# State 4's first decay factor ahead of the silu stretch, the x and dt projections later on TensorE, B rows ahead of C rows, and DRAM pieces of 4 KB

## The chip, the cores and the metric

One NeuronCore of one Trainium2 chip. The metric is the device time of the whole program in microseconds (us), the median of the runs shown.

## The reference, cut to what matters

Four layers over 4096 tokens of 256 channels, each followed by a layer norm. The third is a selective state-space layer of 16 states, and the fourth a feed-forward net; the change is in these two and in the way their input passes through DRAM.

```python
# third layer: x of (tokens, 256)
x_ssm, z = split(x @ w_in.T + b_in)
z = silu(z);  dt = softplus(x_ssm @ w_dt.T + b_dt)
Bm = x_ssm @ w_B.T + b_B;  Cm = x_ssm @ w_C.T + b_C;  A = -exp(A_log)
for t:                                   # for each channel and each of the 16 states
    h = exp(A * dt[t]) * h + dt[t] * Bm[t] * x_ssm[t]
    y[t] = sum(h * Cm[t], axis=states)
x = layernorm(((y + D * x_ssm) * z) @ w_out.T + b_out + x) * gamma + beta, then a plain layernorm
# fourth layer
h = layernorm(x) * ln_gamma + ln_beta
x = layernorm(x + 0.5 * (silu(h @ w1 + b1) @ w2 + b2))
```

## The kernel before, in words

The program runs two layers in stages of their own (functions `first_layer` and `coupling`), and then the third and the fourth together, from about 520 us of the span on. This last stage works in 8 blocks (NB) of 512 tokens (TB). Each engine has its own program, written out by hand as a loop over `it` (L1649 for SP, L1887 for TensorE, L2151 for ScalarE, L2459 for VectorE, L2676 for GpSimd), with `cur = it` the block whose states are scanned now, `post` the one before, `last` and `old` those before that; `nxt` is the one whose projections are prepared. An engine takes its instructions strictly in the order written, and waits at each for the semaphore counts that it names. So the order of these calls is the schedule.

For each of the 16 states n of a block, and each half k of the channels (128 partitions):
- SP loads row n of B and row n of C from the DRAM array `CB_rows`, broadcast to all partitions (`load_B` L1620, `load_C` L1626), into 4 buffers each.
- GpSimd multiplies dt*x with the B row (`into`, L2560, 128x1024).
- ScalarE makes the decay factor exp(A*dt) into a PSUM bank `bank_a0` or `bank_a1` (`decay(b, n, k)`, L2021), copies the C row to a bank (`spread_C`, L2027) and saves the state's last column (`carry`, L2032).
- VectorE runs the recurrence (`scan(b, n, k)`, L2343, 128x512), and multiplies with C (`product(b, n)`, L2350, 128x1024); for n = 0, 12, 14 GpSimd makes that product.
- TensorE adds the products up over the states by transposes into `bank_y` (`add_up(b, n)`, L1762, 8 matmuls).

Besides, for each block, all in one PSUM bank, `single` (named bank_m1), in turn: `x_proj(b, m)` (L1710), evacuated by ScalarE's `evac_x(b, m)` (L2036), for m = 0, 1; `d_proj(b, m)` (L1720) with `evac_d(b, m)` (L2043), twice; `bc_proj` and `evac_bc`; then `z_proj` and `evac_z`, twice. Each projection waits until the one before it is evacuated. TensorE issues x_proj and d_proj of block cur between the add_ups of block post: x_proj(0) after add_up 0, x_proj(1) after 1, d_proj(0) after 2, d_proj(1) after 4. ScalarE has evac_x(0) after decay(4,0), evac_x(1) after decay(5,0), evac_d(0) after decay(6,1), and evac_d(1) at the head of the next turn of its loop (L2154), ahead of decay(8,0). On VectorE product(6) stands after scan(7,0), then come scan(7,1), scan(8,0), two `stats4` of the block before, product(7) and scan(8,1).

The silu stretch of ScalarE (L2263 to L2270) is two silus of the hidden layer `f_h` (128x2048 each), with spread_C(2) between them, and the silu of z; a table load stands ahead of it and one behind. `down_proj` (L1821) on TensorE takes `f_h` in eight parts, between the same add_ups. `stats4` (L2374) on VectorE needs GpSimd's `summed` (L2637), which adds `x2`, the block's input in token order, to the normed output. Into that same `x2` GpSimd's queue has added beta beforehand by a DMA with accumulation (`shifted`, L2577). The input itself goes to DRAM in the stage before, once in token order (`x2_tokens`, L1094) and once by channels (`x2_rows`, L1103), and comes back by `load_x2` (L1607) and `load_xT` (L1602).

## Time and profile before

| what | value |
| --- | --- |
| median of 3 runs | 1088.25 us (1087.13 to 1093.55) |
| profiled execution, its own time | 1091.2 us |
| its span, first to last instruction | 1089.2 us |
| mean granted TensorE clock | 0.966 of full speed |
| instructions | 17899 |

The busy time of an engine is a share of the span; the engines run side by side, so only a wait on the engine that ends a stage last makes the time longer. The numbers of a timeline are: start, duration, engine, line of the kernel, operation, output and input, and in brackets the idle time of the engine just before and what ended it. Durations of neighbours overlap by about 0.1 us, because an engine starts the next instruction while the last one drains. A row with "x2" holds two instructions of one kind, one after the other. The releaser in brackets is inferred.

### The profile page before, as it was taken

The numbers are of one execution on the slowest core, as the hardware profiler recorded it, in microseconds if no ns is written. First come the engines' busy times: TensorE is split into PE (matmuls) and PEld (weight loads), VectorE is DVE, ScalarE is ACT, GpSimd is POOL, SyncE is SP. The second block draws the span as 40 slices with busy tenths as digits, with TensorE's granted clock in tenths as the row PEclk, the third lists the DMA queues.
The fourth block names the chain that finished last, engine by engine and source line by source line (L and its number), as shares of the span: only waits on it lengthen the run. The fifth ranks groups of instructions, "written<-read, shape, count | busy, mean of one in ns | idle before, by whom it ended". The sixth has DMA issues, their size and how long they took to land. (4 is left out here: it accounts for less than half of the span.)

```text
span 1089.2 us, 17899 instructions
## 1 busy us (share of the span) xinstructions
PE 980.9 (90%) x5612; PEld 743.0 (68%) x5612; DVE 929.0 (85%) x1234; ACT 839.4 (77%) x1633; POOL 709.3 (65%) x603
## 2 busy tenths in 40 slices
PE   6999999999978999998668499999999989997987
PEld 4777777777754555555446387777778777886776
DVE  7999999999963797865799898999999899999751
ACT  7778878878746668767877789898998988987733
POOL 2556566766761111223789899999999899999530
PEclk9999999999998999999877799999999999999999
DMA  6543435433415002112998968588786978678301
GB/s 178 145 134 116 135 110 141 122 99 111 126 46 195 0 1 75 43 39 85 244 163 185 141 152 183 129 199 158 162 169 162 168 133 192 171 146 170 86 1 39
DMA packets 97617, 137.53 MB, mean 126 GB/s; under 512 B 8818, under 2 KB 52338, under 8 KB 97524
## 3 DMA queue, kind: packets, MB, share of 16 engines
q1 hardware_dynamic: 93828, 132.73, 50.2%
q0 software_dynamic: 3696, 3.67, 2.8%
q8 instruction: 45, 0.74, 0.3%
q14 instruction: 48, 0.39, 0.2%
HBM read 120.12 MB, written 14.16 MB: 123 GB/s over the span
## 5 line engine op out<-in xcount | busy, mean ns | idle before, releaser
L2348 DVE TENSOR_TENSOR_SCAN oa<-bank_a,h,oa 128x512 f32<-128x512 f32 x128 | 159.8, 1269 | 13.6 <-ACT h L2034 9.7
L2348 DVE TENSOR_TENSOR_SCAN ob<-bank_a,h,ob 128x512 f32<-128x512 f32 x128 | 160.0, 1268 | 8.0 <-ACT bank_a L2025 4.5
L1830 PE MATMUL bank_m<-w,f_h 128*128 128x256 f32 x448 | 104.4, 383 | 0.0
L1491 POOL TENSOR_TENSOR oa<-ob,x1T 128x1024 f32<-128x1024 f32 x8 | 18.8, 2355 | 130.5 <-DVE ob L1391 130.5
L2025 ACT ACTIVATE bank_a<-s,A 128x512 f32<-128x512 f32 x128 | 86.7, 683 | 21.2 <-DVE oa L2348 15.1
L2025 ACT ACTIVATE bank_a<-dtc,A 128x512 f32<-128x512 f32 x128 | 87.0, 684 | 13.7 <-DVE oa L2348 8.1
L1830 PEld LDWEIGHTS bank_m<-w,f_h 128*128 128x128 f32 x448 | 84.4, 192 | 14.1 <-issue 3.6
L1770 PE MATMUL bank_y<-ident,ob 128*128 128x128 f32 x512 | 71.7, 286 | 23.2 <-DVE ob L2354 11.8
L1770 PE MATMUL bank_y<-ident,oa 128*128 128x128 f32 x512 | 72.3, 288 | 17.7 <-DVE oa L2354 17.6
L1770 PEld LDWEIGHTS bank_y<-ident,ob 128*128 128x128 f32 x512 | 62.7, 148 | 34.5 <-DVE ob L2354 14.5
L2568 POOL TENSOR_TENSOR ob<-s,Bb 128x1024 f32<-128x1024 f32 x32 | 76.1, 2378 | 15.0 <-DMA Bb<-CB_rows 10.9
L1770 PEld LDWEIGHTS bank_y<-ident,oa 128*128 128x128 f32 x512 | 63.0, 149 | 29.1 <-DVE oa L2354 21.2
L2568 POOL TENSOR_TENSOR ob<-uc,Bb 128x1024 f32<-128x1024 f32 x32 | 76.1, 2377 | 10.2 <-DMA Bb<-CB_rows 6.5
L673 DVE TENSOR_TENSOR_SCAN L<-abc,zeros,b_id 128x512 f32<-128x512 f32 x64 | 78.3, 1265 | 4.6 <-POOL xd L883 3.6
L2568 POOL TENSOR_TENSOR oa<-uc,Bb 128x1024 f32<-128x1024 f32 x32 | 76.1, 2378 | 9.0 <-DMA Bb<-CB_rows 4.4
L883 POOL TENSOR_TENSOR xd<-xs,L 128x512 f32<-128x512 f32 x32 | 34.0, 1062 | 72.4 <-DVE xs L662 71.9
L2568 POOL TENSOR_TENSOR oa<-s,Bb 128x1024 f32<-128x1024 f32 x32 | 76.1, 2377 | 3.3 <-POOL ob L2575 2.1
L2354 DVE TENSOR_TENSOR oa<-ob,bank_c 128x1024 f32<-128x1024 f32 x64 | 77.3, 1207 | 0.9
L2030 ACT ACTIVATE bank_c<-Cb 128x512 f32<-128x512 f32 x104 | 61.6, 592 | 13.2 <-DVE ob L2354 8.2
L334 PE MATMUL b_op<-W_out,zs 128*128 128x256 f32 x256 | 63.1, 389 | 0.0
L2575 POOL TENSOR_TENSOR ob<-oa,Cb 128x1024 f32<-128x1024 f32 x24 | 57.2, 2383 | 2.7 <-PE bank_y L1770 2.7
L640 DVE SCALAR_TENSOR_TENSOR b_p<-raw,columns,b_p 128x512 f32<-128x512 f32 x72 | 54.2, 753 | 3.3 <-ACT b_p L465 1.7
(405 smaller groups left out, 2912.7 us busy)
## 6 DMA issues: line engine op xcount, KB each, us to landing
Bb<-CB_rows SPq DMA_DIRECT2D x128, 256.0 KB, 6.6
Cb<-CB_rows SPq DMA_DIRECT2D x128, 256.0 KB, 6.4
abc<-decays SPq DMA_DIRECT2D x32, 512.0 KB, 4.5
Ebc<-ramps SPq DMA_DIRECT2D x64, 128.0 KB, 3.1
uT<-in_uT SPq DMA_DIRECT2D x8, 512.0 KB, 4.2
u<-in_u SPq DMA_DIRECT2D x8, 512.0 KB, 3.9
x_tokens<-x2s SPq DMA_DIRECT2D x8, 512.0 KB, 3.2
x_rows<-x1T SPq DMA_DIRECT2D x8, 512.0 KB, 3.0
```

Source lines behind the costliest of these rows:

```text
L334: i = e.matmul(b_op[:, 0:DM], zs[b % 2][:, m, ts], W_out[:, m, :], start=(m == 0), stop=(m == MD - 1))
L640: e.scalar_tensor_tensor(to, raw[:, m, t:t + TB], cw[:, m, t:t + 1], acc[:, :], ALU.mult, ALU.add).then_inc(v_conv, 1)
L673: e.tensor_tensor_scan(L[:, hs, :].rearrange("p h t -> p (h t)"), abc[g % 2][:, hs, :].rearrange("p h t -> p (h t)"), b_id[:, :], zeros[:, ...
L883: e.tensor_tensor(heads(xd[:, :]), heads(xs[g % 2][:, :]), L[:, :, CH - 1:CH].to_broadcast([P, NH, HD]), ALU.mult).then_inc(p_xd, 1)
L1770: i = e.matmul(p_y[c // 2][:, at:at + P], prod[n % 2][:, k, c * CH:(c + 1) * CH], ident[:, :], start=False, stop=(n == NS - 1), is_transpo ...
L1830: i = e.matmul(to, f_h[:, k, c * CH:(c + 1) * CH], w2[:, k, :], start=False, stop=(c % 2 == 1 and k == KF - 1))
L2025: e.activation(p_a[k][:, :], dtc[b % 2][:, k, :], ACT.Exp, scale=A[:, k, n:n + 1]).then_inc(a_a, 1)
L2030: e.activation(p_c[:, :], Cb[n % 4][:, :], ACT.Copy).then_inc(a_c, 1)
L2348: e.tensor_tensor_scan(s[:, k, :], p_a[k][:, :], s[:, k, :], h0[:, n, k:k + 1], ALU.mult, ALU.add).then_inc(v_s, 1)
L2354: e.tensor_tensor(prod[n % 2][:, :, :], state[(NS * b + n) % 4][:, :, :], both(p_c[:, :]), ALU.mult).then_inc(v_g, 1)
L2568: e.tensor_tensor(state[at % 4][:, :, :], uc[b % 2][:, :, :], both(Bb[n % 4][:, :]), ALU.mult).then_inc(p_b, 1)
L2575: e.tensor_tensor(prod[n % 2][:, :, :], state[(NS * b + n) % 4][:, :, :], both(Cb[n % 4][:, :]), ALU.mult).then_inc(p_g, 1)
```

## The change

- **Decay factor.** In blocks 1 to 7 `decay(b, 4, 0)` is written to the bank `single` and issued before the silu stretch (`aside`, `factor`); `scan(b, 4, 0)` reads it there. It waits for the block's last evac_z. `decay(b, 5, 0)`, whose bank that leaves free, waits for scan(3,0) only. `x_proj(b, 0)` waits for that scan of the block before (b > 1).
- **Projections.** On TensorE x_proj(0) comes after add_up(2), x_proj(1) after add_up(3), d_proj(0) after add_up(4), d_proj(1) after add_up(6); the parts of `down_proj` stay where they are between the add_ups. On ScalarE evac_x(0) comes after decay(5,0), and evac_x(1) after decay(5,1); evac_d(0) and evac_d(1) stay.
- **DMAs.** `x2_tokens` and `x2_rows` in DRAM are laid out by partition, so that each partition's share of a block is one piece of 4 KB (before: 1 KB for tokens, 2 KB for rows); beta comes from an array in which it stands 4 times, again 4 KB. On SP load_x2 is issued before store_CB, and load_B(8), (9), (10) each one place earlier, ahead of load_C(6), (7), (8).
- The first fold_beta waits for c_xT, which x_proj did before.

```diff
@@ sync
                         load_C(post, 13)
+                        load_x2(post)
                     if 0 < cur < NB:
                         store_CB(cur)
...
-                    if live(post):
-                        load_x2(post)
...
                         load_B(cur, 7)
+                        load_B(cur, 8)
                         load_C(cur, 6)
-                        load_B(cur, 8)
+                        load_B(cur, 9)
                         load_C(cur, 7)
-                        load_B(cur, 9)
+                        load_B(cur, 10)
                         load_C(cur, 8)
-                        load_B(cur, 10)
                         load_B(cur, 11)
@@ sync, layouts
-                    e.dma_start(xT[:, :, :], x2_rows[:, :, b * TB:(b + 1) * TB]).then_inc(ld_xT, DMAS)
+                    e.dma_start(flat(xT), x2_rows[:, b, :, :].rearrange("p k t -> p (k t)")).then_inc(ld_xT, DMAS)
...
-                    e.dma_start(x2, x2_tokens[:, b * NC:(b + 1) * NC, :]).then_inc(ld_x2, DMAS)
+                    e.dma_start(flat(x2), x2_tokens[:, b, :]).then_inc(ld_x2, DMAS)
@@ new helpers
+            def aside(b, n, k):
+                return b > 0 and (n, k) == (4, 0)
+
+            def factor(b, n, k):
+                return single if aside(b, n, k) else p_a[k]
@@ tensor, x_proj
                         e.wait_ge(a_z, 2 * b)
+                        if b > 1:
+                            e.wait_ge(v_s, 2 * (NS * (b - 1) + 4) + 1)
@@ tensor, order
                         add_up(post, 0)
-                    if 0 < cur < NB:
-                        x_proj(cur, 0)
...
                         add_up(post, 1)
-                    if 0 < cur < NB:
-                        x_proj(cur, 1)
...
                         add_up(post, 2)
                     if 0 < cur < NB:
-                        d_proj(cur, 0)
+                        x_proj(cur, 0)
...
+                    if 0 < cur < NB:
+                        x_proj(cur, 1)
                     if 0 <= old < NB - 2:
                         down_proj(old, 1, 0)
                     if live(post):
                         add_up(post, 4)
                     if 0 < cur < NB:
-                        d_proj(cur, 1)
+                        d_proj(cur, 0)
...
                         add_up(post, 6)
+                    if 0 < cur < NB:
+                        d_proj(cur, 1)
@@ scalar, decay
-                    after(e, v_s, 2 * (NS * b + n - 1) + k + 1)
-                    e.activation(p_a[k][:, :], dtc[b % 2][:, k, :], ACT.Exp, scale=A[:, k, n:n + 1]).then_inc(a_a, 1)
+                    if aside(b, n - 1, k):
+                        e.wait_ge(v_s, 2 * (NS * b + n - 2) + k + 1)
+                    elif aside(b, n, k):
+                        e.wait_ge(a_z, 2 * b + 2)
+                    else:
+                        after(e, v_s, 2 * (NS * b + n - 1) + k + 1)
+                    e.activation(factor(b, n, k)[:, :], dtc[b % 2][:, k, :], ACT.Exp, scale=A[:, k, n:n + 1]).then_inc(a_a, 1)
@@ scalar, order
                         decay(cur, 3, 1)
+                    if 0 < cur < NB:
+                        decay(cur, 4, 0)
                     if 0 <= last < NB - 2:
                         silu_up(last, 0)
...
                         silu_z(cur)
-                    if live(cur):
+                    if cur == 0:
                         decay(cur, 4, 0)
+                    if live(cur):
+                        decay(cur, 4, 1)
                         carry(cur, 2)
+                        spread_C(cur, 3)
+                        carry(cur, 3)
+                        decay(cur, 5, 0)
                     if live(nxt):
                         evac_x(nxt, 0)
-                    if live(cur):
-                        decay(cur, 4, 1)
-                        spread_C(cur, 3)
-                        carry(cur, 3)
-                    if live(cur):
-                        decay(cur, 5, 0)
-                    if live(nxt):
-                        evac_x(nxt, 1)
                     if live(cur):
                         carry(cur, 4)
                         spread_C(cur, 4)
                         decay(cur, 5, 1)
+                    if live(nxt):
+                        evac_x(nxt, 1)
```

## Rows read from the trace of the kernel before

**Rows 1.** The page, busy times: us, share of the span, instructions.
```profile
PE 980.9 (90%) x5612; PEld 743.0 (68%) x5612; DVE 929.0 (85%) x1234; ACT 839.4 (77%) x1633; POOL 709.3 (65%) x603
```

**Rows 2.** Table by stretches, two blocks: length, busy per engine, clock, DMA.
```profile
719.30:782.70 63.40, 59.90 (x347) 48.86 (x346) 60.74 (x61) 57.35 (x103) 59.88 (x38) 1.00 0.79 164
846.20:911.50 65.30, 60.06 (x346) 48.73 (x345) 60.69 (x60) 57.30 (x102) 59.50 (x38) 1.00 0.85 163
```

**Rows 3.** VectorE's waits in the blocks from 719.3 and from 846.2.
```profile
DVE oa L2348 <- ACT h L2034: 1.4, 1, 1.4
...
DVE st L2376 <- POOL xl L2641: 2.5, 1, 2.5
```

**Rows 4.** Timeline of VectorE: scan(4,·), product(3), scan(6,0), product(6), scan(7,1), scan(8,0).
```profile
726.64 2.56 DVE L2348 TENSOR_TENSOR_SCAN oa<-bank_a,h,oa 128x512 f32<-128x512 f32 x2 [1.41 <-ACT h L2034]
729.12 1.20 DVE L2354 TENSOR_TENSOR oa<-ob,bank_c 128x1024 f32<-128x1024 f32 x1
...
733.73 1.26 DVE L2348 TENSOR_TENSOR_SCAN oa<-bank_a,h,oa 128x512 f32<-128x512 f32 x1
...
738.39 1.20 DVE L2354 TENSOR_TENSOR ob<-oa,bank_c 128x1024 f32<-128x1024 f32 x1
739.94 1.28 DVE L2348 TENSOR_TENSOR_SCAN ob<-bank_a,h,ob 128x512 f32<-128x512 f32 x1 [0.35 <-POOL ob L2568]
741.14 1.27 DVE L2348 TENSOR_TENSOR_SCAN oa<-bank_a,h,oa 128x512 f32<-128x512 f32 x1
```

**Rows 5.** Timeline of ScalarE: decay(3,·), silu, decay(4,0), decay(5,1), norm3, decay(7,1), evac_d(1).
```profile
716.71 1.30 ACT L2025 ACTIVATE bank_a<-s,A 128x512 f32<-128x512 f32 x2
...
719.32 1.92 ACT L2103 ACTIVATE f_h<-f_h 128x2048 f32<-128x2048 f32 x1
...
725.82 0.69 ACT L2025 ACTIVATE bank_a<-s,A 128x512 f32<-128x512 f32 x1
...
730.95 0.67 ACT L2025 ACTIVATE bank_a<-s,A 128x512 f32<-128x512 f32 x1
731.56 1.08 ACT L2077 ACTIVATE xl<-xl,nb,rs 128x256 f32<-128x256 f32 x2
...
739.14 0.67 ACT L2025 ACTIVATE bank_a<-s,A 128x512 f32<-128x512 f32 x1
739.75 0.66 ACT L2049 ACTIVATE dtc<-bank_m,columns 128x512 f32<-128x512 f32 x1
```

**Rows 6.** Timeline of TensorE: x_proj(1), add_up(2), d_proj(1), add_up(6).
```profile
727.26 1.98 PE L40 MATMUL bank_m<-s,w_xz 128*128 128x512 f32 x4 [1.41 <-ACT xc L2041]
729.08 1.04 PE L1770 MATMUL bank_y<-ident,ob 128*128 128x128 f32 x8
...
737.04 1.88 PE L40 MATMUL bank_m<-xc,w_dt 128*128 128x512 f32 x4
...
741.37 1.04 PE L1770 MATMUL bank_y<-ident,ob 128*128 128x128 f32 x8
```

**Rows 7.** Stretch of TensorE alone: length, busy, granted clock, DMA share, GB/s.
```profile
605.40:608.60 3.20, 3.18 (x4) 0.56 0.69 127
```

**Rows 8.** Timeline of TensorE, d_proj(1) in the block from 592.
```profile
605.42 3.37 PE L40 MATMUL bank_m<-xc,w_dt 128*128 128x512 f32 x4 [2.32 <-ACT dtc L2049]
```

**Rows 9.** Timeline of VectorE, stats4 in the block from 592.
```profile
616.36 1.30 DVE L2376 BATCH_NORM_STATS2 st<-xl 128x6 f32<-128x512 f32 x2 [4.85 <-POOL xl L2641]
```

**Rows 10.** Timeline of GpSimd, into(9) in the block from 592.
```profile
611.68 2.34 POOL L2568 TENSOR_TENSOR ob<-s,Bb 128x1024 f32<-128x1024 f32 x1 [3.42 <-DMA Bb<-CB_rows]
```

**Rows 11.** Timeline of VectorE, product(6) and scan(8,0) in the block from 532.
```profile
549.41 1.20 DVE L2354 TENSOR_TENSOR ob<-oa,bank_c 128x1024 f32<-128x1024 f32 x1
...
551.78 1.27 DVE L2348 TENSOR_TENSOR_SCAN oa<-bank_a,h,oa 128x512 f32<-128x512 f32 x1
```

**Rows 12.** DMA issues of the page: engine, count, KB each, median us to landing.
```profile
x_tokens<-x2s SPq DMA_DIRECT2D x8, 512.0 KB, 3.2
x_rows<-x1T SPq DMA_DIRECT2D x8, 512.0 KB, 3.0
```

More of the change, by code:

```diff
@@ L1012, in build @@
         ld_B, ld_C = [d_sem(f"ld_B{i}") for i in range(4)], [d_sem(f"ld_C{i}") for i in range(4)]
-        x2_tokens, x2_rows = scratch["x2_tokens"].rearrange("(n p) f -> p n f", p=P), rows(scratch["x2_rows"])
+        x2_tokens, x2_rows = scratch["x2_tokens"], scratch["x2_rows"]
         c_row, c_tok = new_sem("c_row"), [new_sem("c_tok0"), new_sem("c_tok1")]
@@ L1093, in sync @@
                     e.wait_ge(c_n, 4 * b + 4)
-                    e.dma_start(x2_tokens[:, b * NC:(b + 1) * NC, :], x2s[b % 2][:, :, :]).then_inc(c_tok[b % 2], DMAS)
+                    e.dma_start(x2_tokens[:, b, :], x2s[b % 2][:, :, :].rearrange("p c f -> p (c f)")).then_inc(c_tok[b % 2], DMAS)
                     if b == NB - 3:
@@ L1102, in sync @@
                     e.wait_ge(c_xT, 2 * b + 2)
-                    e.dma_start(x2_rows[:, :, tokens(b)], x1T[:, :, tokens(b)]).then_inc(c_row, DMAS)
+                    e.dma_start(x2_rows[:, b, :, :], x1T[:, :, tokens(b)]).then_inc(c_row, DMAS)
                     if b == NB - 2:
@@ L1539, in both @@
                 return x.rearrange("p (o t) -> p o t", o=1).to_broadcast([P, KD, TB])
-            beta_row = d["everywhere"].rearrange("(a o n) -> a o n", a=1, o=1)[:, :, sum(n for _, n in EVERYWHERE) - DM:]
+            beta_row = d["beta_rows"].rearrange("(a n) -> a n", a=1)
             def rowwise(v):
@@ L1746, in fold_beta @@
                 def fold_beta(part):
+                    if part == 0:
+                        e.wait_ge(c_xT, 2 * NB)
                     for m in (2 * part, 2 * part + 1):
@@ L2270, in scalar @@
                         silu_z(cur)
+                    if cur == 0:
+                        decay(cur, 4, 0)
                     if live(cur):
-                        decay(cur, 4, 0)
+                        decay(cur, 4, 1)
                         carry(cur, 2)
+                        spread_C(cur, 3)
+                        carry(cur, 3)
+                        decay(cur, 5, 0)
                     if live(nxt):
                         evac_x(nxt, 0)
-                    if live(cur):
-                        decay(cur, 4, 1)
-                        spread_C(cur, 3)
-                        carry(cur, 3)
-                    if live(cur):
-                        decay(cur, 5, 0)
-                    if live(nxt):
-                        evac_x(nxt, 1)
                     if live(cur):
@@ L2347, in scan @@
                     s = state[(NS * b + n) % 4]
-                    e.tensor_tensor_scan(s[:, k, :], p_a[k][:, :], s[:, k, :], h0[:, n, k:k + 1], ALU.mult, ALU.add).then_inc(v_s, 1)
+                    e.tensor_tensor_scan(s[:, k, :], factor(b, n, k)[:, :], s[:, k, :], h0[:, n, k:k + 1], ALU.mult, ALU.add).then_inc(v_s, 1)
                 def product(b, n):
@@ L2578, in shifted @@
                     e.wait_ge(v_pre, 2 * b + 2)
-                    e.dma_start(x2, beta_row.to_broadcast([P, NC, DM]), accum_op=ALU.add).then_inc(ld_beta, DMAS)
+                    e.dma_start(flat(x2), beta_row.to_broadcast([P, NC * DM]), accum_op=ALU.add).then_inc(ld_beta, DMAS)
                 def scales(parts, done, base):
@@ L2778 @@
         "columns": np.concatenate([column(down[n]) for n, _ in COLUMNS], axis=1),
+        "beta_rows": np.tile(a[L1 + "beta"], NC),
         "everywhere": np.concatenate([every[n].reshape(-1) for n, _ in EVERYWHERE]),
@@ L2784 @@
     out = nc.dram_tensor("out", (T, DM), F32, kind="ExternalOutput").ap()
-    scratch = {n: nc.dram_tensor(n, shape, F32, kind="Internal").ap() for n, shape in (("x2_tokens", (T, DM)), ("x2_rows", (DM, T)), ("CB_rows", (2 * NS, T)), ("decays", (NB * NC, DT, CH)), ("ramps", (NB * NC, DT, CH)))}
+    scratch = {n: nc.dram_tensor(n, shape, F32, kind="Internal").ap() for n, shape in (("x2_tokens", (P, NB, NC * DM)), ("x2_rows", (P, NB, KD, TB)), ("CB_rows", (2 * NS, T)), ("decays", (NB * NC, DT, CH)), ("ramps", (NB * NC, DT, CH)))}
     build(nc, dram, out, scratch)
```

## The prediction

> **What bounds the kernel now.** The whole page comes first: VectorE is busy for 85% of the span [rows 1], but that is a mean over four layers, and all of the reordering lies in the last one, which starts at about 520 us. So the second view is the table by stretches. One block of that layer (512 tokens) takes 63.4 us, and in it TensorE works 59.9, VectorE 60.7, ScalarE 57.4 and GpSimd 59.9 us [rows 2]. Four engines are nearly full; the longest, VectorE, has only 2.7 us to spare. The block from 846 us is 1.9 us longer. The third view, VectorE's waits, says where: 1.4 us before `scan(4,0)` in every block, and 2.5 us before `stats4` in the long one [rows 3].
>
> Fourth, the timelines of one block, that of 719 us. VectorE is idle for 1.41 us before the two scans of state 4 at 726.64 [rows 4]. ScalarE's row explains it: from 718.0 it is in the silu stretch (a table load, two silus of `f_h`, the silu of z, a table load back) and only at 725.82 does it write state 4's first decay factor [rows 5]. It hardly rests afterwards. The second small wait of VectorE, 0.35 us before `scan(7,1)` at 739.94, is put down to GpSimd, but the scan starts 0.13 us after ScalarE ends `decay(7,1)` (739.14 + 0.67), so it is ScalarE's. Fifth, TensorE [rows 6]: `x_proj(1)` at 727.26, `d_proj(1)` at 737.04, `add_up(6)` at 741.37. The four projections share one bank with their evacuations: x_proj(0), evac_x(0), x_proj(1), evac_x(1), d_proj(0), evac_d(0), d_proj(1), evac_d(1), strictly in turn. Now `d_proj(1)` is complete at 738.9 and ScalarE takes it at 739.75: 0.8 us in hand. That chain is what the change moves later.
>
> **The decay factor.** `decay(4,0)` goes ahead of the silus. It needs a slot of 0.61 us on ScalarE, so all up to its old place is 0.61 us later, and `decay(4,1)` starts at 726.44 and ends at 727.13. `scan(4,0)` goes at 725.2 (726.64 - 1.41), ends 726.5; `scan(4,1)` waits until 727.26; `product(3)` starts at 728.45 instead of 729.12. This part alone gives 0.67 us, not 1.41. It can't give more by `scan(7,1)`: from 718 to 739.8 ScalarE has 0.62 us of idle time, and its work isn't less.
>
> **The x and d projections.** The sum, for the same block; a semaphore from VectorE to TensorE or ScalarE costs 0.03 to 0.09 us, ScalarE to VectorE 0.13, a projection delivers 2.0 us after its first matmul when it had to wait (1.98 in [rows 6]), an `add_up` takes 0.87 in a full stream, eight matmuls of `down_proj` 1.73.
> Step 1: `x_proj(0)` now waits for `scan(4,0)`: it starts at 726.5 and delivers at 728.5; `evac_x(0)` ends at 729.15. ScalarE had got there at 728.4: nothing lost yet.
> Step 2: TensorE does `down_proj(0,1)` to 730.0, `add_up(3)` to 730.9 (product(3) is there at 729.7), then `x_proj(1)`, delivered at 732.95.
> Step 3: ScalarE, in order, reaches `evac_x(1)` at 730.9 and stands for 2.05 us. Behind it stand norm3, decay(6,0), and all else: norm3 starts at 733.54 instead of 731.56 [rows 5]. `decay(6,0)` ends at 735.2, and `scan(6,0)` starts at 735.33 instead of 733.73: the gain is gone and 1.6 us are lost.
> Step 4: ScalarE has no slack to 739.8, so it stays 2.0 late: `product(6)` at 740.26 instead of 738.39, ending 741.47. `d_proj(0)`, after `add_up(4)`, delivers at 737.37, when ScalarE just gets there: no further loss.
> Step 5: `d_proj(1)` now stands behind `add_up(6)`, which needs product(6): 741.53, then 0.87, then 2.05 to deliver (744.45), `evac_d(1)` 0.57, `decay(8,0)` 0.68, 0.13. `scan(8,0)` starts at 745.84 instead of 741.14: 4.7 us per block. The reason is one of order: ScalarE has `evac_d(1)` ahead of `decay(8,0)`, and on VectorE only one scan lies between product(6) and scan(8,0). From the end of product(6) the round trip is 4.35 us, the scan covers 1.2.
>
> After scan(8,0) the order and the gaps are as before; the two waits left (0.5 us at the softplus, 0.2 at the gate) follow VectorE and stay.
>
> By blocks: the one of 532 us (no silu_up, no new wait): the x loop makes product(6) about 1.1 us late and the round trip adds 3.2 (scan(8,0) was 2.37 after product(6) [rows 11]), 4.3; less 0.3 for earlier B rows, 4.0. The one of 592: scan(8,0) would come at 615.3 and end at 616.5, but VectorE waited for stats4 until 616.36 anyway, 4.85 us [rows 9]: of the loss 0.7 is left (scan(9,1), which follows the softplus). Those of 656, 719, 782 and 911: 4.7 each, 18.8. The one of 846: its wait of 2.5 us for stats4 vanishes and the 0.5 at the softplus returns: 4.7 - 2.0 = 2.7. The last, 975, has no projections to come: it keeps the first part, -0.5. Sum: 4.0 + 0.7 + 18.8 + 2.7 - 0.5 = 25.7 us.
>
> **The DMAs.** Rows of B ahead of C: GpSimd stood 3.42 us for Bb before `into(9)` in the block of 592 [rows 10], which made most of the 4.85. Both this and the 2.5 us are covered by the new lateness, so I cost the order at nothing; without that cover it would give up to 4.85 + 2.5. `load_x2` moves ahead of `store_CB` and of the first B rows on SP; its semaphores are long up there, its issue takes some 0.4 us, and the first B rows of the next block then have half a megabyte less in front of them. Larger pieces: half a megabyte of 1 KB pieces lands in 3.2 us and one of 2 KB in 3.0 [rows 12]; doubling gave 0.2. One more doubling or two on x2, xT and beta, none of which ended a wait but beta's perhaps in `summed`: 0 taken, bounds -2 (the 532 block, where GpSimd waits for B behind these stores) and +0.5 (if longer pieces hold a ring against the B rows). The Trainium skill, page "DMA: Bandwidth & Descriptors", section Specifications, asks for pieces of at least 512 B for line rate; by that the change of pieces would be worth nothing at all, while the row gives the 0.2 us per doubling. The sum is the same with either.
>
> **Sum and its base.** The profiled execution took 1091.2 us (span 1089.2): 1091.2 + 25.7 = 1116.9. The median of the runs is 2.95 us lower, so the forecast is 1088.25 + 25.7 = 1114 us, up 2.4%.
>
> **The rivals.**
> First, the wait goes and the projections stay hidden. Per block 0.6 x 6, and the stats4 waits go too (4.85 + 1.9), and 1 us of DMA: -11.3, 1077 us. For it: 1.41 us of idle time is plain to see. Against it: `d_proj(1)` cannot start before product(6), and decay(8,0) stands behind it in ScalarE's program. It would need the round trip to be under 1.2 us, and the rows say 4.35.
> Second, only the last loop costs. If TensorE brings x_proj(1) in time (from about 731 on), step 3 falls away; product(6) would be up to 0.6 us early, scan(8,0) at 743.3: 2.1 per block, 0.1 in that of 846, 2.6 in the first: +10.6, 1099 us. For it: TensorE's ends are modelled. Against: add_up(3) can't start before product(3), 729.7, and the rest is 2.9 us of work.
> Third, TensorE's clock falls besides. After the new round trip TensorE has caught up and stands about 2.5 us before `add_up(8)`. In the block of 592 it stood for 2.32 us, and the four matmuls after took 3.37 us [rows 8] where 1.98 is usual, at a mean granted clock of 0.56 [rows 7], that is mostly at 1.2 GHz. That costs up to 1.4 us of TensorE's time per block, in a stretch where it also waits for others; if it all counts in 6 blocks, +8.4: 1122 us. Against: at 752 to 755 it also idles today and the clock stays. The Trainium skill, "TensorE: Matmul & The Clock Gate", section What's actually happening, says that the slow clock is the default and that activity lifts it; by it the same would happen after each new pause.
>
> **How the numbers follow.** Forecast 0.63; clock 0.17; last loop only 0.15; hidden 0.05. The range leaves out the last case and the edges: 1098 to 1124. About 1% (10.9 us) is what this kernel's measurement can tell from no change. Faster by over 1%: 0.04, from the hidden case. Within 1%: 0.06, from a third of "last loop only" and a little of hidden. Slower by over 1%: 0.90.
>
> **What would show it.** In the profile after: blocks of about 68 us from 656 on; no wait before scan(4,0); a new idle of ScalarE of about 2 us before xc (evac_x(1)) and of about 2.7 us before dtc (evac_d(1)), both released by TensorE; VectorE waiting about 2.3 us before scan(6,0) and 2.7 before scan(8,0); no wait for xl in stats4. Wrong, if ScalarE takes evac_d(1) without a wait, or if the blocks stay at 63 us.

## The result, and the profile after

The kernel after takes 1125.88 us (median of 4 runs, 1124.15 to 1126.19) against 1090.38 us of the kernel before (1087.13 to 1093.55): ratio 1.032, 95% interval [1.0296, 1.0344]. It is slower by 35.5 us. The forecast was 1114 us with a range of 1098 to 1124: the direction was right, but a rise of 25.7 us was forecast and 35.5 was measured. (The median lies 11.9 us above the forecast. 2.1 us of that come from its base, the median of three runs; a fourth run of the kernel before moved it from 1088.25 to 1090.38.)

The page of the kernel after: its span, and the busy times that answer to [rows 1].

```profile
span 1123.2 us, 17899 instructions
...
PE 999.5 (89%) x5612; PEld 751.9 (67%) x5612; DVE 930.8 (83%) x1234; ACT 838.2 (75%) x1633; POOL 705.4 (63%) x603
```

The work of VectorE and ScalarE is that of before to 2 us; they stand longer. TensorE is the one with more busy time (999.5 against 980.9 us) for the same 5612 instructions, so some of them ran slower. The table by stretches (length, busy time with count of TensorE, its weight loads, VectorE, ScalarE and GpSimd, granted clock, DMA share, GB/s) for the first three blocks and three later ones; the fourth and the sixth row answer to the two of [rows 2]:

```profile
532.50:599.90 67.40, 49.28 (x251) 39.35 (x250) 54.96 (x51) 42.63 (x78) 49.93 (x22) 0.75 0.74 164
599.90:671.90 72.00, 56.20 (x296) 42.48 (x295) 62.07 (x58) 55.32 (x99) 60.79 (x42) 0.86 0.67 148
671.90:741.00 69.10, 63.22 (x346) 50.77 (x345) 59.91 (x59) 55.27 (x99) 56.95 (x35) 0.95 0.58 146
...
741.00:808.90 67.90, 62.34 (x346) 49.83 (x345) 60.95 (x61) 57.42 (x103) 58.27 (x37) 0.97 0.67 157
808.90:876.80 67.90, 62.25 (x346) 49.52 (x345) 60.94 (x61) 57.41 (x103) 58.27 (x37) 0.97 0.66 155
876.80:946.20 69.40, 63.74 (x347) 50.98 (x346) 61.34 (x61) 57.41 (x104) 58.22 (x37) 0.95 0.65 152
```

A usual block (those from 741.00, 808.90 and 946.20 here) is 67.9 us instead of 63.4. VectorE's busy time in it is unchanged (60.95 against 60.74), so the 4.5 us are waiting. Where it waits, the view of its waits says (us in total, times, longest), block from 808.9; [rows 3] had 1.4 us before scan(4,0) here:

```profile
DVE oa L2363 <- ACT bank_a L2039: 4.6, 2, 2.5
DVE ob L2363 <- ACT bank_a L2039: 1.1, 2, 0.5
DVE oa L2363 <- ACT h L2048: 0.9, 1, 0.9
DVE zgs L2375 <- PE bank_y L1779: 0.2, 1, 0.2
```

The timelines give each its place. VectorE: scan(6,0), product(6), scan(7,1), scan(8,0), as in [rows 4].

```profile
820.08 1.28 DVE L2363 TENSOR_TENSOR_SCAN oa<-bank_a,h,oa 128x512 f32<-128x512 f32 x1 [2.08 <-ACT bank_a L2039]
...
824.94 1.22 DVE L2369 TENSOR_TENSOR ob<-oa,bank_c 128x1024 f32<-128x1024 f32 x1
826.67 1.28 DVE L2363 TENSOR_TENSOR_SCAN ob<-bank_a,h,ob 128x512 f32<-128x512 f32 x1 [0.51 <-ACT bank_a L2039]
830.47 1.28 DVE L2363 TENSOR_TENSOR_SCAN oa<-bank_a,h,oa 128x512 f32<-128x512 f32 x1 [2.51 <-ACT bank_a L2039]
```

ScalarE: evac_x(1), evac_d(0), evac_d(1), as in [rows 5].

```profile
817.71 0.69 ACT L2055 ACTIVATE xc<-bank_m,columns 128x512 f32<-128x512 f32 x1 [1.90 <-PE bank_m L40]
...
822.10 0.68 ACT L2063 ACTIVATE s<-bank_m,columns 128x512 f32<-128x512 f32 x1
...
829.07 0.69 ACT L2063 ACTIVATE s<-bank_m,columns 128x512 f32<-128x512 f32 x1 [2.53 <-PE bank_m L40]
```

TensorE: add_up(6), d_proj(1) and add_up(8), as in [rows 6].

```profile
826.21 1.09 PE L1779 MATMUL bank_y<-ident,ob 128*128 128x128 f32 x8 [0.86 <-DVE ob L2369]
827.14 1.88 PE L40 MATMUL bank_m<-xc,w_dt 128*128 128x512 f32 x4
...
839.43 1.57 PE L1779 MATMUL bank_y<-ident,ob 128*128 128x128 f32 x8 [2.39 <-DVE ob L2369]
```

Read from product(6): VectorE writes it from 824.94 to 826.16, TensorE adds it up at once, projects to 829.02, ScalarE evacuates at 829.07 and makes the decay factor at 829.65, and VectorE, which has only scan(7,1) to do meanwhile, has stood 2.51 us when it starts scan(8,0) at 830.47. Two round trips that were hidden before are now on the path: this one, and that through x_proj(1), for which ScalarE stands 1.90 us. scan(4,0) itself no longer waits; the 0.9 us in the view of the waits stand before scan(4,1).

Per block, measured from the start of one silu of z to the next (the last entry runs to the end of the span), the kernels compared below have these lengths. The labels are those of the experiments. The blocks have the names that they have in the prediction; from 656 on the silu of z starts some 4 us behind the name (at 660.5, 723.5 and so on in the kernel before). The columns 719, 782 and 846 are the blocks from 741.0, 808.9 and 876.8 of the kernel after. Each row is one profiled execution, so a difference that shows in one row alone may be one of executions.

```
kernel       532    592    656    719    782    846    911  975 to end   span
before      59.40  68.25  62.97  63.42  63.43  65.37  63.43  110.1     1089.2
after       67.37  71.98  69.14  67.89  67.90  69.33  67.92  109.1     1123.2
e1_order    69.79  71.33  67.96  68.18  68.15  68.17  68.17  110.1     1126.1
e2_dma      63.49  64.00  62.95  63.40  63.42  63.40  63.41  110.0     1088.4
e3_d1       65.33  67.64  64.18  65.30  65.28  65.29  65.30  109.0     1101.3
e4_fill     69.50  75.64  67.41  67.90  67.92  67.90  67.88  108.9     1125.5
e5_first    61.28  64.34  67.40  67.90  67.90  67.90  67.89  110.6     1108.5
e6_x1       63.83  65.40  63.55  65.30  65.30  65.31  65.29  109.0     1095.6
e7_pieces   63.42  63.95  62.96  63.42  63.40  63.42  63.40  110.3     1088.2
e8_sp       62.79  65.38  62.95  63.41  63.42  63.41  63.42  111.7     1089.1
e9_tight    59.66  65.24  62.63  63.43  63.44  63.44  63.44  109.1     1083.0
e10_fill    67.12  67.75  67.41  67.91  67.90  67.91  67.91  110.5     1116.9
```

### The profile page after: what moved, and what is told of

It reads as the page before. It is cut to its first block and busy times, and to the rows that moved or that the text cites. A ratio compares the mean times of both kernels' runs of the same rounds, so it can differ in the third digit from the quotient of the medians.

```text
span 1123.2 us, 17899 instructions
## 1 busy us (share of the span) xinstructions
PE 999.5 (89%) x5612; PEld 751.9 (67%) x5612; DVE 930.8 (83%) x1234; ACT 838.2 (75%) x1633; POOL 705.4 (63%) x603
## 2 busy tenths in 40 slices
DMA packets 87889, 137.53 MB, mean 122 GB/s; under 512 B 8818, under 2 KB 40562, under 8 KB 87796
## 5 line engine op out<-in xcount | busy, mean ns | idle before, releaser
L2363 DVE TENSOR_TENSOR_SCAN oa<-bank_a,h,oa 128x512 f32<-128x512 f32 x121 | 151.5, 1272 | 45.9 <-ACT bank_a L2039 34.2
L1779 PE MATMUL bank_y<-ident,ob 128*128 128x128 f32 x512 | 76.4, 298 | 44.6 <-DVE ob L2369 33.1
L1779 PEld LDWEIGHTS bank_y<-ident,ob 128*128 128x128 f32 x512 | 64.3, 153 | 57.6 <-DVE ob L2369 41.4
L2039 ACT ACTIVATE bank_a<-s,A 128x512 f32<-128x512 f32 x124 | 84.1, 685 | 14.4 <-DVE oa L2363 8.8
L1779 PE MATMUL bank_y<-ident,oa 128*128 128x128 f32 x512 | 75.5, 296 | 19.9 <-DVE oa L2369 19.5
L1779 PEld LDWEIGHTS bank_y<-ident,oa 128*128 128x128 f32 x512 | 64.3, 153 | 35.8 <-DVE oa L2369 32.8
```

The lines of the kernel that those rows point to most:

```text
L1779: i = e.matmul(p_y[c // 2][:, at:at + P], prod[n % 2][:, k, c * CH:(c + 1) * CH], ident[:, :], start=False, stop=(n == NS - 1), is_transpo ...
L2039: e.activation(factor(b, n, k)[:, :], dtc[b % 2][:, k, :], ACT.Exp, scale=A[:, k, n:n + 1]).then_inc(a_a, 1)
L2363: e.tensor_tensor_scan(s[:, k, :], factor(b, n, k)[:, :], s[:, k, :], h0[:, n, k:k + 1], ALU.mult, ALU.add).then_inc(v_s, 1)
```

## The experiments

They ran in three series (e1 to e4, e5 to e8, e9 and e10), each on another chip and each with runs of the kernel before among them. Every ratio is against the kernel before of its own series.

**The order of the projections alone (e1_order).** The kernel before with the projections later on TensorE and ScalarE; decay(4,0) stays behind the silus, no bank is borrowed, the DMAs are as before.

```diff
                         add_up(post, 0)
-                    if 0 < cur < NB:
-                        x_proj(cur, 0)
...
                         add_up(post, 2)
                     if 0 < cur < NB:
-                        d_proj(cur, 0)
+                        x_proj(cur, 0)
...
                         add_up(post, 6)
+                    if 0 < cur < NB:
+                        d_proj(cur, 1)
```

> The kernel before with the later x and dt projections alone (TensorE's and ScalarE's order of them; no decay factor in the shared bank, DMAs as before). Theory 1, the order of the projections makes the whole loss: about 5 us per full block (4.7, and 0.35 more because product(3) is later without the early factor), as much in the first block as after the change: 1127 us (1120 to 1132). Rival, the loss comes from the shared bank, x_proj(0) waiting for scan(4,0): under 1100 us.

Measured: 1126.27 us (before in these runs 1092.6), ratio 1.0312, interval [1.0279, 1.0345]. The order makes the whole loss; the shared bank and the DMAs are not needed for it. Its usual block is 68.17 us, 0.27 longer than that of the kernel after: that is all that the early factor is worth there (the DMA parts, the other difference, leave the usual block at 63.4, see e2_dma). As the expectation said, the first block loses at least as much as after the whole change, 10.4 us against 8.0.

**The DMA parts alone (e2_dma).** New layouts, beta array and SP's order, nothing else.

```diff
-                    e.dma_start(x2, x2_tokens[:, b * NC:(b + 1) * NC, :]).then_inc(ld_x2, DMAS)
+                    e.dma_start(flat(x2), x2_tokens[:, b, :]).then_inc(ld_x2, DMAS)
```

> The kernel before with the DMA parts alone (4 KB pieces, rows of B ahead of C, load_x2 earlier). Theory 1: nothing is lost, and without the cover of the late projections the waits of stats4 in the blocks of 592 and 846 us go, 4.8 and 1.9 us: 1083 us (1080 to 1090). Rival 2, that the excess of 3.4 us in the block of 532 us over the forecast is GpSimd waiting longer for B (3.69 us after, 2.93 before, ahead of into(4)): 1092 us or more, and that wait over 3.5 us.

Measured: 1088.42 us, ratio 0.9961, interval [0.9943, 0.998]. The waits for stats4 went in both places (68.25 to 64.00, 65.37 to 63.40), but the first block became 4.1 us longer (59.40 to 63.49). GpSimd waits longer there before into(4), for the first row of B that was not loaded in the stage before. This is its timeline in this kernel; the wait was 2.93 us in the kernel before:

```profile
537.44 2.35 POOL L2567 TENSOR_TENSOR oa<-uc,Bb 128x1024 f32<-128x1024 f32 x1 [4.24 <-DMA Bb<-CB_rows]
```

So of the rival the wait came true (over 3.5 us) and the time did not. Over the first two blocks the sum is that of before (127.5 against 127.7), and only the 2 us of the block from 846 are left; in this execution the first block also starts 1.4 us later.

**d_proj(1) ahead of the trip through product(6) (e3_d1).** The kernel after, with that one projection two places earlier.

```diff
                         add_up(post, 5)
+                    if 0 < cur < NB:
+                        d_proj(cur, 1)
...
                         add_up(post, 6)
-                    if 0 < cur < NB:
-                        d_proj(cur, 1)
```

> The kernel after, with d_proj(1) ahead of add_up(6) (behind add_up(5)). Theory 1, the round trip through product(6): ScalarE no longer stands before evac_d(1) (2.5 us now), the full blocks shrink from 67.9 to 65.2 us, the first two by about 3 as well: 1107 us (1103 to 1112). If the loss were in x_proj(1) alone: within 3 us of the kernel after.

Measured: 1103.09 us, ratio 1.0093, interval [1.0062, 1.0125]. The usual block falls from 67.9 to 65.3, as expected to 0.1. The span falls by 21.9 us, more than 2.6 per block, because the blocks from 592, 656 and 846 shrink by 4.3, 5.0 and 4.0 us; that from 532 shrinks by 2.0.

**x_proj(1) earlier besides (e6_x1).** As e3_d1, and

```diff
+                    if 0 < cur < NB:
+                        x_proj(cur, 1)
                     if live(post):
                         add_up(post, 3)
...
                     if 0 <= post < NB - 1:
                         norm3(post, 0)
+                    if live(nxt):
+                        evac_x(nxt, 1)
```

> The kernel after with d_proj(1) behind add_up(5) (as in the run e3_d1), and besides x_proj(1) ahead of add_up(3) on TensorE, with evac_x(1) behind the first norm3 on ScalarE. My theory: the loss of 4.5 us per full block has two terms, the trip through product(6), which the earlier run took away (67.9 to 65.3), and ScalarE's stand of 1.9 us before evac_x(1), which this one takes away: full blocks at 63.4 (63.0 to 63.8), 1103.1 - 5 x 1.9 = 1093.6 (1090 to 1098). Rival: the remaining 1.9 us is TensorE's lower clock and its dips, or ScalarE's stand moves on to evac_d(0); then the blocks stay at 65 or more and the time above 1100.

Measured: 1097.4 us, ratio 1.0032, interval [1.0017, 1.0046]. A miss: the usual block stays at 65.3. ScalarE's wait for x_proj(1) is gone, but ScalarE's timeline shows what took its place, the next link of the chain, evac_d(0):

```profile
803.87 0.69 ACT L2063 ACTIVATE s<-bank_m,columns 128x512 f32<-128x512 f32 x1 [1.78 <-PE bank_m L40]
```

1.90 us of waiting became 1.78, because d_proj(0) still stood behind a part of down_proj and add_up(4). It was the second half of the rival, though the time stayed under its 1100. Of the 5.7 us that were gained 4.4 are in the first three blocks; the rest is in front of them, where this execution starts its first block 1.4 us earlier.

**Each projection as early as the borrowed bank allows (e9_tight).** All parts of the change; order of before in the first two blocks; from the third on, against the kernel after,

```diff
                         down_proj(old, 0, 1)
+                    if 2 < cur < NB:
+                        x_proj(cur, 1)
                     if live(post):
                         add_up(post, 3)
...
-                    if 0 < cur < NB:
-                        x_proj(cur, 1)
+                    if 2 < cur < NB:
+                        d_proj(cur, 0)
...
                         add_up(post, 4)
                     if 0 < cur < NB:
-                        d_proj(cur, 0)
+                        d_proj(cur, 1)
```

> All parts of the change, but the projections brought only as late as the borrowed bank forces: the first two blocks in the order of before (factor of block 1 in its old place); from the third on x_proj(0) behind add_up(2), x_proj(1) behind the next part of down_proj and ahead of add_up(3), d_proj(0) behind add_up(3), d_proj(1) behind add_up(4); evac_x(1) on ScalarE behind the first norm3. The run with d_proj(1) and x_proj(1) moved had blocks of 65.3 us, with ScalarE standing 1.78 us for d_proj(0) and VectorE 1.67 us before scan(7,0). My theory: that stand is the last one of the chain; with d_proj(0) one add_up earlier ScalarE no longer waits and the early factor's gain of 0.6 us per block comes out: full blocks 62.8 (62.6 to 63.4), first two 61.3 and 64.3 as in the run e5_first; 1111.5 - 5 x 5.1 = 1086 us (1083 to 1090) against about 1092 of before, ratio 0.994. Rival: the early factor gives nothing, since ScalarE's work in the block is the same and VectorE's waits only move; then the blocks take 63.4 or more and the time is 1089 or more, no better than the DMA parts alone.

Measured: 1087.96 us (12 runs; before in these 1090.1), ratio 0.9977, interval [0.9961, 0.9993]. The loss is gone: in the usual block ScalarE waits for no x or dt projection by more than 0.2 us. But that block is 63.44, not 62.8. So the two waits for projections together carry the 4.5 us of the usual block, and the gain by the early factor, 0.6 us per block in my sum, does not exist: the rival was right, and the kernel is no better than the DMA parts alone (0.9961). VectorE's waits in the usual block, here from 786:

```profile
DVE ob L2378 <- ACT bank_a L2045: 1.1, 2, 0.5
DVE oa L2378 <- ACT h L2054: 0.9, 1, 0.9
DVE oa L2378 <- ACT bank_a L2045: 0.2, 1, 0.2
DVE zgs L2390 <- PE bank_y L1779: 0.2, 1, 0.2
```

They add up to 2.4 us; before, the same view of the block from 786.9 has 1.4, 0.5, 0.4 and 0.2, 2.5 in all. The 1.4 us before scan(4,0) are spread over scan(4,1) (0.86), scan(6,0) (0.23) and scan(7,1) (0.51 instead of 0.35).

**The old order in the first two blocks only (e5_first).** The kernel after, in which the projections of blocks 1 and 2 stand as before.

```diff
                         add_up(post, 0)
+                    if cur in (1, 2):
+                        x_proj(cur, 0)
...
-                    if 0 < cur < NB:
+                    if 2 < cur < NB:
                         x_proj(cur, 0)
```

> The kernel after, in which only the projections that run beside the first two blocks of the last stage (those of blocks 1 and 2) keep the order of before, on TensorE and ScalarE, and block 1's factor stays in its old place. The two blocks take 67.4 and 72.0 us in the kernel after; with the DMA parts alone they take 63.5 and 64.0. My theory: what my forecast missed lies in these two blocks, and it is the chain of the projections that starts later there, so they return to about 63.5 and 64.0 and all others stay as in the kernel after: 1125.9 - 3.9 - 8.0 = 1114 us (1110 to 1118). Rival: the excess of the two blocks is TensorE's cold start or the DMAs and not the order; then they stay at 66 to 72 and the time is above 1120.

Measured: 1111.46 us, ratio 1.0165, interval [1.0137, 1.0194]. Expected 1114. The two blocks return to 61.3 and 64.3, 13.7 us in all, so what they lost came with the order too. Besides, the block from 656 takes 67.40 instead of 69.14, at a granted clock of 1.00 instead of 0.95, and that from 846 67.90 instead of 69.33, at 0.97 instead of 0.95, though nothing was changed in them: those 1.4 to 1.7 us are not the order itself, and can be there in one execution and not in another.

**A filled TensorE, first try (e4_fill).** The kernel after with 8 dummy passes ahead of add_up(0) in the first block and 8 ahead of add_up(2) in the second.

```diff
+                    if cur == 2:
+                        e.wait_ge(v_pre, 2)
+                        fill(pair[1], 8)
                     if live(post):
                         add_up(post, 2)
```

> The kernel after with 8 matmuls of 128x512 added on TensorE ahead of add_up(0) of the first block and 8 more ahead of add_up(2) of the second, into banks not read before the next start; they only keep TensorE busy where it stood 5.85 and 1.94 us. Theory 3, the excess of the first two blocks over the forecast (3.4 and 3.0 us) is TensorE at 1.2 GHz in the projections: those blocks shrink by 3 to 6 us in all, x_proj(0) of the second block takes 1.9 instead of 3.4 us, 1121 us (1118 to 1123). Rival, the excess is the order itself at any clock: within 1 us of the kernel after.

Measured: 1130.49 us, ratio 1.0343, interval [1.0309, 1.0378]. A miss, and no answer: the dummies were far too long. TensorE's timeline of this kernel shows those of the second block; x_proj(0), which took 3.46 and 3.41 us in the two blocks of the kernel after, took 1.88 in the first here:

```profile
603.97 7.03 PE L1763 MATMUL bank_m<-w_xz 128*128 128x512 f32 x16
```

7 us of filler in a gap of 1.94 us cost more than the clock gave, and so did 9.4 us in the gap of the first block, where d_proj(1) then ran slowly instead (3.20 us). Behind the second block there are no dummies, and still the blocks from 656 and 846 take 67.4 and 67.9 us at a clock of 1.00, after the same pause of 2.39 us before add_up(8) as in the kernel after.

**The same with two dummies in each of the gaps (e10_fill).** Ahead of add_up(8) from the second block on, and in the second block ahead of add_up(2) and add_up(6).

```diff
+                    if 1 < cur < NB:
+                        e.wait_ge(a_d, 2 * cur + 2)
+                        fill(single, 2)
                     if live(post):
                         add_up(post, 8)
```

> The kernel after with two dummy passes (512 columns each, into a bank that is free then, results not used) ahead of add_up(8) in the blocks from the second on, where TensorE stands 2.4 us, and in the second block also ahead of add_up(2) (stood 1.9 us) and add_up(6) (stood 2.4 us). Theory: the 1.2 to 1.4 us by which the blocks of 672 and 877 exceed the usual 67.9 (69.1 and 69.3, granted clock 0.95 in both) and some 3 us of the second block (its d_proj(1) took 3.6 us instead of 1.9) are TensorE's lower clock after such idle stretches; filled, the clock stays, those blocks come to 67.9 and 69 to 70: 1125.9 - 5.5 = 1120 us (1118 to 1123). Rival: the clock falls off the path; the time stays within 1 us of 1125.9.

Measured: 1120.13 us (before in these runs 1090.1), ratio 1.0277, interval [1.0254, 1.03]. Work was added, and against the kernel before the ratio is 1.0277 where the kernel after had 1.032 (the intervals share 0.0004). The stretches of the blocks from 592, 656 and 846:

```profile
599.60:667.40 67.80, 57.39 (x309) 42.04 (x308) 62.12 (x58) 55.36 (x99) 60.83 (x42) 0.95 0.69 157
667.40:734.80 67.40, 62.33 (x351) 49.33 (x349) 59.61 (x59) 55.44 (x100) 56.94 (x35) 1.00 0.59 150
870.60:938.50 67.90, 62.58 (x351) 49.44 (x350) 60.95 (x60) 57.48 (x104) 58.25 (x37) 1.00 0.65 154
```

They are 4.2, 1.7 and 1.4 us shorter than in the kernel after, at clocks of 0.95, 1.00 and 1.00 instead of 0.86, 0.95 and 0.95. For the block from 592 the dummies are the likely cause: x_proj(0), d_proj(1) and the add_ups between them are all fast in it. For the other two it is not shown, because these blocks had the short length and the full clock in e4_fill too, without a dummy. What speaks for the dummies there is that in all four runs the mean clock of the whole span is 0.965 to 0.967, while it is 0.951 to 0.953 in the four of the kernel after.

**The pieces alone, and SP's order alone (e7_pieces, e8_sp).** The two halves of e2_dma, each on the kernel before.

```diff
-            beta_row = d["everywhere"].rearrange("(a o n) -> a o n", a=1, o=1)[:, :, sum(n for _, n in EVERYWHERE) - DM:]
+            beta_row = d["beta_rows"].rearrange("(a n) -> a n", a=1)
```

> The kernel before with the new DRAM layouts (4 KB pieces for x2, xT and beta) alone, without the new order of SP. The DMA parts together made the first block 4.1 us longer (GpSimd's wait for the first B rows went from 2.9 to 4.2 us) and took away the waits for stats4 in the blocks of 592 and 846. The changed order of SP cannot act before the first B rows, so my theory: the first block's 4 us come from the pieces, 63.5 us here, and the block of 592 stays within 1 us of 68; 1092 + 4 = 1094 us (1090 to 1098). Rival: the pieces also take the waits away, and this kernel is as fast as both together, 1088.

```diff
                         load_C(post, 13)
+                        load_x2(post)
...
+                        load_B(cur, 8)
                         load_C(cur, 6)
-                        load_B(cur, 8)
```

> The kernel before with SP's order alone (load_x2 ahead of store_CB and of the first B rows; B rows 8, 9 and 10 one place earlier), old DRAM layouts. My theory: the first block stays at 59.4 to 60 us, and the waits before stats4 in the blocks of 592 and 846 go: 68.3 to 64 and 65.4 to 63.4. 1090.4 - 6 = 1084 us (1081 to 1088), ratio 0.994. Rival: the first block loses its 4 us here too, so they belong to the queue's order or to chance, and the time is 1088.

Measured: pieces 1088.61 us, ratio 0.9947 [0.9929, 0.9965]; SP's order 1090.03 us, ratio 0.9966 [0.9948, 0.9983]; before in these runs 1094.56. Both expectations failed in part. The pieces alone take both waits for stats4 away, which I had put down to SP's order; against the kernel before of their series they give 5.9 us. SP's order alone takes away the wait of the block from 846 and about halves the other. What is left of its 4.8 us, in the view of VectorE's waits, with the pieces alone:

```profile
DVE st L2376 <- POOL xl L2641: 0.2, 1, 0.2
```

With SP's order alone:

```profile
DVE st L2375 <- POOL xl L2640: 2.7, 1, 2.7
```

And the first block is longer in both, 63.4 and 62.8, so it isn't the pieces as such. What makes it 59.4 in the kernel before, 59.7 in e9_tight (which has all the DMA parts) and about 63 in the three DMA kernels was not settled. The traces differ in one more thing there: in e2_dma and e7_pieces, but not in e8_sp, e9_tight or the kernel before, TensorE stood 1.5 us before the block's x_proj(0) for its load from `x2_rows`. In the three DMA kernels the second block is short where the first is long. The two gains do not add: both together gave 0.9961.

## Why the prediction was right in direction and wrong in size

The forecast's terms against what was measured, in us over the kernel before; the third column is e10_fill, in whose trace most of the drops of the clock are missing.

```
block          forecast   after   e10_fill
532                4.0      8.0       7.7
592                0.7      3.7      -0.5
656                4.7      6.2       4.4
719, 782, 911      4.7 each 4.5 each  4.5 each
846                2.7      4.0       2.5
975 to the end    -0.5     -1.0       0.4
start of the first  -      -0.3      -0.4
sum               25.7     34.0      27.7
```

The forecast failed in two terms. The x loop of the first block was put at 1.1 us and measured 4.5; and TensorE's clock, put at nothing in the sum, made most of what the blocks from 592, 656 and 846 are above it (3.0, 1.5 and 1.3 us). The rest of the sum was too high by 1.4 us.

- **The bound and the two round trips (steps 1 to 5): right.** 4.7 us were forecast, 4.5 measured. By single waits: 2.05 us before evac_x(1), measured 1.90; 2.7 before evac_d(1), 2.53; about 2.3 before scan(6,0), 2.08; 2.7 before scan(8,0), 2.51; about 2.5 of TensorE before add_up(8), 2.39. e3_d1 took the second trip away, for 2.6 of the 4.5 us; e9_tight took away the rest. (That scan(4,0) waits 1.4 us "in every block" is not so: the view of the waits has 2.6 us in the block from 656 and no such wait in the first two. The sum of 656 did not suffer by it.)
- **The term that failed most in size: the block from 532, "the x loop makes product(6) about 1.1 us late and the round trip adds 3.2", 4.0.** The block lost 8.0. VectorE's timeline in it, kernel after:

```profile
553.65 1.19 DVE L2369 TENSOR_TENSOR ob<-oa,bank_c 128x1024 f32<-128x1024 f32 x1
...
559.12 1.28 DVE L2363 TENSOR_TENSOR_SCAN oa<-bank_a,h,oa 128x512 f32<-128x512 f32 x1 [3.02 <-ACT bank_a L2039]
```

  The block starts at 532.55 here and started at 532.84 before, so product(6) comes 21.1 us behind the start instead of 16.6 [rows 11]: 4.5 us late, not 1.1. From it to scan(8,0) are 5.5 us instead of 2.4: the round trip adds 3.1, as forecast. So it is the x loop that was mis-sized; I took its slack from the usual block. ScalarE stood for x_proj(0), x_proj(1) and d_proj(1) in turn:

```profile
543.35 0.69 ACT L2055 ACTIVATE xc<-bank_m,columns 128x512 f32<-128x512 f32 x1 [3.92 <-PE bank_m L40]
...
547.60 0.69 ACT L2055 ACTIVATE xc<-bank_m,columns 128x512 f32<-128x512 f32 x1 [2.37 <-PE bank_m L40]
...
557.74 0.69 ACT L2063 ACTIVATE s<-bank_m,columns 128x512 f32<-128x512 f32 x1 [4.37 <-PE bank_m L40]
```

  That is 10.7 us of standing, where the kernel before had 3.2 for the projections in this block (2.1 before xc and 1.1 before s in the view of ScalarE's waits). The longest of the first two, 3.92 us, is for x_proj(0). TensorE had stood 5.85 us for GpSimd's product(0) and starts add_up(0) only at 531.39. In the new order two more add_ups and two parts of `fold_beta` (small matmuls that come in this block alone) stand ahead of x_proj(0), and TensorE does them all at the lower of its two levels. Its stretch from there to the end of x_proj(0), kernel after (granted clock 0.51):

```profile
531.40:543.10 11.70, 11.70 (x46) 9.75 (x46) 7.58 (x7) 6.21 (x9) 6.56 (x3) 0.51 0.98 217
```

  x_proj(0) starts at 539.76 instead of 533.78. The 0.3 us that I took off for earlier B rows did not come either: GpSimd waits 3.69 us before into(4) instead of 2.93. How much of this wait the clock makes and how much the order, no run separates: e4_fill had the fast clock there but delayed the add_ups by its own dummies. With the old order and the same DMA parts product(6) comes 16.8 us behind the start in e5_first, but 20.7 in e2_dma, where GpSimd waits longer for its row of B. So the order's share of the 8.0 is not known to better than the 4 us by which this block differs among kernels that have the old order in it (59.4 to 63.5 us).
- **The clock: "Third, TensorE's clock falls besides" was a rival at 0.17, and it came true in part, on top of the forecast.** It was priced at up to 1.4 us in each of 6 blocks. Between the traces of the kernel after and of e10_fill lie 4.2 us in the block from 592, 1.7 in that from 656, 1.4 in that from 846 and nothing in the other full blocks. (The first block, whose slow stretch is the one above, got no dummies in e10_fill.) So the forecast for the block from 592 (0.7) failed by the clock: in e10_fill that block is 0.5 us shorter than before. TensorE's timeline there, kernel after:

```profile
619.45 1.97 PE L1779 MATMUL bank_y<-ident,ob 128*128 128x128 f32 x8 [2.39 <-DVE ob L2369]
621.21 3.62 PE L40 MATMUL bank_m<-xc,w_dt 128*128 128x512 f32 x4
```

  add_up(6) and d_proj(1), both inside the new round trip, take 5.4 us instead of the 2.8 of the usual block (826.21 to 829.02), and ScalarE, VectorE and scan(8,0) wait for all of it. Elsewhere the drop comes after add_up(8), off the path, and costs only where it lasts. Stretches of the kernel after: behind add_up(8) in the block from 808.9 and in that from 876.8.

```profile
839.40:843.20 3.80, 3.66 (x28) 2.48 (x28) 3.80 (x7) 3.27 (x7) 3.04 (x2) 0.57 0.70 154
907.30:914.70 7.40, 6.84 (x43) 5.46 (x44) 7.40 (x10) 5.89 (x14) 6.41 (x4) 0.56 0.73 215
```

  Both are near the lower level of 1.2 GHz; 3.8 us of it cost nothing (block 67.9), 7.4 us cost 1.4 (block 69.4). By the Trainium skill, "TensorE: Matmul & The Clock Gate", section What's actually happening, the slow clock is the default and activity lifts it. The trace agrees that a pause can bring it (1.9 to 2.4 us here) and that in the block from 592 the fast one stayed where the pauses were filled; it does not agree that each pause does: before add_up(8) in the block from 656 (2.38 us) the next eight matmuls still took 1.09 us, and the first slow ones began 2.7 us later; in e1_order and e4_fill no matmul behind the same pause of 2.39 us was slow, in this block or in that from 846.
- **The decay factor, "this part alone gives 0.67 us": wrong.** It gave 0.27 in the kernel after (68.17 to 67.90) and nothing in e9_tight, where nothing covers it. (No run has the early factor alone.) The wait of 1.41 us was no slack to be had. The factor costs ScalarE the same 0.6 us ahead of the silus as behind them: decay(7,1) starts 15.68 us after the silu of z in the kernel before and 15.07 in e9_tight, and the difference is the 0.61 us by which the silu itself now comes later. ScalarE's later work comes when it came, and what VectorE doesn't wait before scan(4,0) it waits before the next scans. Whether the last block's -0.5 is real can't be told: the end of the span takes 109.1 us in the kernel after and 110.6 in e5_first, whose programs are the same there.
- **"Both are covered by the new lateness": right for the kernel after**, which has no wait for stats4; alone, the DMA parts give 0.4%. But the bounds for the pieces, "-2 and +0.5", were too narrow: alone they give 5.9 us (e7_pieces, interval 3.8 to 7.8), and the second block is 4.3 us shorter and the first 4.0 longer with them.
- **The first rival (hidden) and the second (last loop only)** are out: evac_x(1) waited 1.90 us, and the whole is +3.2%, where they gave 1077 and 1099 us.

The spans differ by 34.0 us and the medians by 35.5; the difference lies within the spread of the runs of before (6.4 us).

## What to carry to other kernels

When several producers and consumers take turns in one buffer, moving the first of them later moves all of them. Price each link by when its consumer's engine gets there, and do this again for the blocks at the start, whose slack is another than that of the usual block. A wait of one engine on another in a loop of two (here VectorE's 1.41 us on ScalarE) isn't slack if the work that is moved stays on the engine that makes the other wait. And a new round trip through TensorE must be priced at both levels of the clock where TensorE has paused just before it: here its two groups of matmuls took 5.4 us in one block and 2.8 in the others.

## What the runs showed of the hardware that was not expected

- A filled gap can pay: with two dummy passes (1.88 us at the fast clock) in each of three gaps of 1.9 to 2.4 us the block from 592 is 4.2 us shorter (71.98 to 67.75), though TensorE does more work in it.
- After the same pause of 2.39 us the low clock lasted 3.8 us, 7.4 us, or did not come at all (stretches above, and e1_order and e4_fill), so its cost is not one number per pause. It can't be read from one execution either.
- With pieces of 4 KB the page counts 87889 DMA packets instead of 97617 for the same 137.53 MB. The loads back, which queue among the broadcasts of B and C, land sooner. In the kernel before they take 7.1 (tokens) and 5.6 us (rows); with the pieces alone (e7_pieces), by the DMA issues:

```profile
s<-x_tokens SPq DMA_DIRECT2D x8, 512.0 KB, 6.4
s<-x_rows SPq DMA_DIRECT2D x7, 512.0 KB, 4.3
```

  With SP's order alone and the old pieces (e8_sp) they take 8.6 and 4.6 us, so for the rows part of the gain is open to the order as well. The stores take 2.7 and 3.6 us in e7_pieces against 3.2 and 3.0 [rows 12]: one shorter, one longer.

I had sized the pieces by the stores, 0.2 us per doubling, and so missed the loads.
